# Tiles 4 to 7 of a folded adapter-and-expert layer: each pair's product with the folded weights made of seven block products instead of eight

## The reference

```python
h      = x @ W + (x @ lora_A[idx]) @ lora_B[idx]          # per tile, rank 16
out    = h @ W_base.T + b_base
logits = h @ W_gate.T                                     # 8 experts
p      = top-2 of softmax(logits), made to sum to 1; route_w puts it back on 8 experts
delta  = ((h @ A[e].T) * route_w[e]) @ B[e].T, summed over e   # rank 16 per expert
result = x + out + delta
```

## Time and profile before

| | us |
|---|---|
| median of 3 runs (lowest, highest) | 65.82 (65.64, 66.08) |
| span of the profiled execution, first to last instruction | 64.2 |
| TensorE busy | 60.7 |
| VectorE busy | 36.7 |
| ScalarE busy | 25.7 |
| GpSimd busy | 17.9 |
| granted TensorE clock, share of full speed | 1.00 |

### The profile page before, as it was taken

How to read it: one execution, slowest core, us unless ns; L and a number is a source line. 1 busy time by engine, 2 the same in 40 slices (tenths; PEclk the granted TensorE clock), 3 DMA queues, 4 the chain that set the end, 5 groups by cost and what they waited for, 6 DMA issues and landing times.

```text
span 64.2 us, 1268 instructions
## 1 busy us (share of the span) xinstructions
PE 60.7 (95%) x418; PEld 59.6 (93%) x418; DVE 36.7 (57%) x131; ACT 25.7 (40%) x73; POOL 17.9 (28%) x41
## 2 busy tenths in 40 slices
PE   4979999999999999999999999999999999999950
PEld 4969999999999999999999999999999999999940
DVE  0948599915799747020788748990477240467120
ACT  1752899507294270001163436611272011173620
POOL 1000899899988802030020301230000000000000
DMA  0799999702988102232332323800017000008044
GB/s 0 209 328 308 367 406 411 278 3 48 323 295 309 31 0 42 61 70 60 70 70 57 63 66 65 309 31 5 0 48 278 0 10 0 0 28 299 0 163 163
DMA packets 5048, 8.46 MB, mean 132 GB/s; under 512 B 1057, under 2 KB 1569, under 8 KB 5042
## 3 DMA queue, kind: packets, MB, share of 16 engines
q1 hardware_dynamic: 4370, 7.57, 36.6%
q0 software_dynamic: 384, 0.56, 2.4%
q10 hardware_dynamic: 288, 0.27, 1.2%
HBM read 5.26 MB, written 2.10 MB: 115 GB/s over the span
## 4 chain that ended last, share of the span: by engine, by line
PE 90%; DMA 5%; ACT 1%; issue 0%
PE bank L487 22%; PE bank L489 22%; PE bank L488 22%; PE bank L495 8%; PE bank L497 6%; DMA w_raw<-fold_in 5%; PE bank L573 2%; PE bank L538 2%; PE bank L554 2%; PE bank L544 2%; PE bank L577 1%; PE bank L528 1%; ACT y_out L333 1%; PE bank L584 1%; PE bank L588 1%
## 5 line engine op out<-in xcount | busy, mean ns | idle before, releaser
L487 PE MATMUL bank<-cl_hi,x_hi 128*128 128x408 f32 x32 | 11.4, 356 | 0.0
L489 PE MATMUL bank<-cl_hi,x_lo 128*128 128x408 f32 x32 | 11.2, 349 | 0.0
L488 PE MATMUL bank<-cl_lo,x_hi 128*128 128x408 f32 x32 | 11.1, 348 | 0.0
L487 PE MATMUL bank<-cr_hi,x_hi 128*128 128x256 f32 x32 | 9.6, 301 | 0.0
L489 PE MATMUL bank<-cr_hi,x_lo 128*128 128x256 f32 x32 | 9.0, 282 | 0.0
L488 PE MATMUL bank<-cr_lo,x_hi 128*128 128x256 f32 x32 | 9.0, 282 | 0.0
L261 POOL CAST cl_hi<-lora_raw 128x64 fp32r<-128x64 f32 x8 | 1.9, 239 | 16.8 <-PE bank L489 16.8
L448 DVE MAX8 top_val<-bank 128x8 f32<-128x8 f32 x8 | 1.4, 169 | 8.7 <-PE bank L538 8.7
L487 PEld LDWEIGHTS bank<-cr_hi,x_hi 128*128 128x128 f32 x32 | 6.1, 190 | 0.2
L228 POOL DMA_DIRECT2D lora_raw<-lora x8 | 4.5, 564 | 6.2 <-issue 6.1
L487 PEld LDWEIGHTS bank<-cl_hi,x_hi 128*128 128x128 f32 x32 | 6.0, 188 | 0.1
(11 more groups left out here) (99 smaller groups left out, 149.3 us busy)
## 6 DMA issues: line engine op xcount, KB each, us to landing
x_raw<-x_t SPq DMA_DIRECT2D x8, 256.0 KB, 4.5
out<-y_out SPq DMA_DIRECT2D x7, 256.0 KB, 2.1
w_raw<-fold_in SPq DMA_DIRECT2D x4, 256.0 KB, 5.1
w_raw<-fold_in SPq DMA_DIRECT2D x3, 324.0 KB, 5.2
bw_rows<-bw_hi SPq DMA_DIRECT2D x16, 40.5 KB, 2.0
lora_raw<-lora POOLq DMA_DIRECT2D x8, 64.0 KB, 3.9
bw_rows<-bw_lo SPq DMA_DIRECT2D x8, 40.5 KB, 2.1
ffn_b_raw<-ffn_b SPq DMA_DIRECT2D x1, 256.0 KB, 6.1
```

The lines of the kernel that those rows point to most:

```text
L487: nc.tensor.matmul(out, a_hi, b_hi, start=first, stop=False, skip_group_check=True)
L488: nc.tensor.matmul(out, a_hi, b_lo, start=False, stop=False, skip_group_check=True)
L489: return nc.tensor.matmul(out, a_lo, b_hi, start=False, stop=last, skip_group_check=True)
```

## The change

Pairs 2 and 3 (tiles 4, 5 and 6, 7) are multiplied by Strassen's scheme. For a pair with tiles a and b, the features are cut in halves 1 and 2 and the output columns in halves, so that `[a1 a2; b1 b2]` meets `[B11 B12; B21 B22]`. `M5 = (a1+a2) B22`, `M4 = b2 (B21-B11)`, `M3 = a1 (B12-B22)`, `M2 = (b1+b2) B11`, `M1 = (a1+b2)(B11+B22)`, `M6 = (b1-a1)(B11+B12)`, `M7 = (a2-b2)(B21+B22)`. Each is two chunks of three matmuls. M5, M4, M3, M2 carry the gate, h and adapter columns along (408 columns, in the left banks); M1, M6, M7 have 256 columns. Tile a's left bank now holds the right half of its output.

The operands that this needs are made on the chip. ScalarE copies the raw folded weights out of the banks (`copy_left_raw`, `copy_right_raw`), VectorE makes the differences `X4` and `X3`, GpSimd the sums `SUM1`, `SUM7`, `SUM6` (`sum_c`), the mixed x quarters (`sum_x`: three of 256 columns, and then one of 512 in place), and the adapters' A columns for a pair (`split_la_pair`). All are split into hi and lo. The results are combined with copies of M5 and M4 and with sums `e`, `z`, `u1`, `u2` and `add_u` on GpSimd and VectorE. The bias moves from GpSimd to ScalarE and VectorE, and its rows go out as eight DMAs on SyncE's queue.

```diff
+SEVEN = (2, 3)
+X5, X3, C01, C23, X4 = range(5)
+SUM1, SUM6, SUM7 = range(3)
...
+            def sum_x(q):
+                x, k = quarters(x_raw, q), SEVEN.index(q)
+                pool.wait_ge(x_loaded[2 * q], DMA)
+                pool.wait_ge(x_loaded[2 * q + 1], DMA)
+                pool.wait_ge(x_lo_done, 4)
+                nc.gpsimd.tensor_tensor(x_mix[k][:, SUM1], x[:, 0], x[:, 3], ALU.add).then_inc(x_mixed, 1)
+                nc.gpsimd.tensor_tensor(x_mix[k][:, SUM6], x[:, 2], x[:, 0], ALU.subtract).then_inc(x_mixed, 1)
+                nc.gpsimd.tensor_tensor(x_mix[k][:, SUM7], x[:, 1], x[:, 3], ALU.subtract).then_inc(x_mixed, 1)
+                pool.wait_ge(x_mixed, 3 * k + 3)
+                nc.gpsimd.tensor_tensor(x[:, 1:3], x[:, 1:3], x[:, 0:4:3], ALU.add).then_inc(x_summed, 1)
...
+            def split_x_inner(q):
+                act.wait_ge(x_summed, SEVEN.index(q) + 1)
+                nc.scalar.copy(quarters(x_hi, q)[:, 1:3], quarters(x_raw, q)[:, 1:3]).then_inc(x_hi_done, 1)
...
+            copy_xa_t(3)
+            copy_left(4)
+            copy_right(4)
+            exp_top(6)
+            copy_left(5)
+            copy_right(5)
+            exp_top(7)
+            split_hw(6)
+            split_hw(7)
...
+            gate(6)
+            sum_u1(3)
+            gate(7)
+            split_hw(6)
+            split_hw(7)
...
+            def M4(q):
+                pe.wait_ge(yl_done, 2 * q - 2)
+                if q == SEVEN[0]:
+                    pe.wait_ge(x4_lo_done, 1)
+                seven_left(2 * q + 1, 2, X4, q, True).then_inc(m4_done, 1)
+
+            def M3(q):
+                if q == SEVEN[0]:
+                    pe.wait_ge(x3_lo_done, 1)
+                    pe.wait_ge(x3_gh_done, 2)
+                pe.wait_ge(m5_copied, SEVEN.index(q) + 1)
+                seven_left(2 * q, 0, X3, q, False).then_inc(left_done, 1)
...
             Lora_left(1)
-            Left(4, ALL)
+            M5(2)
+            M4(2)
             T2(2)
-            Left(5, ALL)
+            M3(2)
+            M2(2)
             T2(3)
...
+            M7(2)
+            T1(3)
+            M6(2)
+            Lora_left(3)
+            Lora_right(2, (4, 5))
+            Delta(4)
+            M1(3)
+            Delta(5)
+            M7(3)
+            T2(6)
+            M6(3)
+            Lora_right(3, (6, 7))
+            T2(7)
+            Delta(6)
+            Delta(7)
```

More of the change, by code:

```diff
@@ L170, in right, with quarters, xd, xd_chunk @@
             return right_bank[t % 2][:, 0:HALF]
+        def quarters(x, q):
+            return x[:, 2 * q:2 * q + 2].rearrange("p t (h c) n -> p (t h) (c n)", h=2)
+        def xd(x, q):
+            return quarters(x, SEVEN.index(q))[:, 0:3]
+        def xd_chunk(x, q, which, c):
+            return xd(x, q)[:, which, c * P:(c + 1) * P]
+        def xd_free(q):
+            return 2 * SEVEN.index(q) + 1
+        def mix(q):
+            return part(x_flat, 2 * q * D, 3, HALF)
+        def la_slot(q):
+            return slice(0, R) if q % 2 == 0 else slice(OWN, OWN + R)
+        def la_own(q):
+            return own_cols(q)
         def fold_right(i):
@@ L244, in gpsimd_program, with split_la @@
             pool.wait_ge(even_zeros, 1)
[L246 to L258, removed]
+            def split_la(t):
                 if t >= 2:
@@ L287, in scalar_program @@
             split_x(1)
+            act.wait_ge(bias_loaded, DMA)
+            nc.scalar.copy(bias_hi[:], bias_raw[:]).then_inc(bias_hi_done, 1)
             act.wait_ge(lora_loaded, NT * DMA)
@@ L298, in scalar_program @@
                 nc.scalar.copy(cl_hi[:, i, LORA_LEFT], bank[i][:, 0:LEFT]).then_inc(cl_hi_done, 1)
[L299 to L303, removed]
+            act.wait_ge(cr_summed, 1)
+            nc.scalar.copy(cr_hi[:].rearrange("p c n -> p (c n)"), bank[4][:]).then_inc(cr_hi_done, 1)
@@ L518, in Right, with seven_left @@
                         pe.wait_ge(cr_lo_done, c // 2 + 1)
-                    product(right(t), x_hi[:, t, c, :], x_lo[:, t, c, :], cr_hi[:, c, :], cr_lo[:, c, :], c == 0, False)
+                    b_hi = cr_hi[:, c, :] if c < 2 else c_hi[:, X5, c - 2, A_RIGHT]
+                    b_lo = cr_lo[:, c, :] if c < 2 else c_lo[:, X5, c - 2, A_RIGHT]
+                    product(right(t), x_hi[:, t, c, :], x_lo[:, t, c, :], b_hi, b_lo, c == 0, False)
+            def seven_left(t, c0, which, q, first):
+                own = la_own(q)
+                for c in range(2):
+                    mm = product(left(t)[:, own], x_hi[:, t if which in (X5, X3) else 2 * q + 1, c0 + c, :],
+                                 x_lo[:, t if which in (X5, X3) else 2 * q + 1, c0 + c, :],
+                                 c_hi[:, which, c, own], c_lo[:, which, c, own], first and c == 0, False)
+                return mm
```

479 lines of the change are left out of this document (385 added, 94 removed).

## The result

The changed kernel took a median of 71.65 us (71.10 to 72.57, 4 runs) where the kernel before, beside it, took 65.73 (65.07 to 66.08, 4 runs): a ratio of 1.096, 95% interval 1.085 to 1.108. The forecast was 67.2 us in a range of 65.5 to 68.4: the sign was right, the loss was more than four times the one forecast, and the time lies outside the range. The profiled execution took 71.1 us with a span of 69.9, so its rows are compared with those of the 64.2 us span of before.

The account below looks back on a forecast made before the run. The number of matmuls on TensorE was taken as the bound. Twelve fewer (-1.44 us) plus A 1.6, B 0.43, C 0.15, D 0.55, E 0.14 gave +1.43 on 65.82: 67.2 us, range 65.5 to 68.4.

Parts of the forecast that it names:

- term A: First adapter product: ScalarE's adapter rows stand behind a cast waiting for GpSimd's x sums, slowed by VectorE's subtractions; +1.6 us.
- Term D: Transpose T2 of tile 7 at the end: later exponential of tile 6 and a new sum between gates; +0.55 us.
- B: M4 of tiles 4 and 5 waits for tile 1's left half to be copied out of its bank; +0.43 us.
- C: M3 of tiles 4 and 5 waits for ScalarE's copy of M5, behind tile 3's exponential; +0.15 us.
- E: After T2 of tile 7, only Delta of tile 6 stands before tile 7's low part is needed; +0.14 us.
- Rival 2: GpSimd is held up and slow at 2.9 ns a column, making A 2.8 us: 68.5 us; chance 0.15.

Follow-up runs that it names:

- the faster kernel: Changed kernel with gate steps moved off SBUF-only operands, GpSimd's weight sums out of the first gates, and lists reordered: 64.61 us (0.983), again 64.13 (0.985).
- sums alone: Kernel before plus three unread GpSimd sums of 512 columns, started when the first adapter product is done: 69.47 us against 65.45.
- the same sums beside the other gate: Kernel before plus the same three unread GpSimd sums, with the one-hot made from and in the bank and no difference step: 65.66 us, 1.006.
- The run with the end's old order: Changed kernel with tile 6's exponential ahead of the copy of tile 4's right half, and `u1` behind `split_hw(6)`: 70.87 us, 1.087.
- order alone: Seven-product kernel with every list in the order of the faster kernel, but with the old gate: 66.39 us, 1.021.

## Why the prediction was wrong

**The bound and the matmuls were right.** TensorE's matmuls set the time, and twelve of them are worth 1.44 us: the faster kernel shows 1.65 between its first and last tile product. (The pages count 418 and 406 matmuls, not 412 and 400; the difference is the forecast's.)

**The step that failed is in term A's second half: "After it, GpSimd's list goes on ... sums for the weights".** It asked only whether those sums are ready for the products that read them. It did not ask which VectorE instructions run beside them, though the same text knew that the two engines disturb each other, and it priced that as a share of time lost by GpSimd (0.57 us per us), never as a delay of VectorE. The row that it rested on the earlier trace rows shows both sides: the subtraction that lasted 0.95 instead of 0.68 us was taken as a reason to lower the price, and not as a price of its own. A share of overlap also hides the size: a step of 0.17 us that starts just behind the start of a sum of 1.27 costs 1 us, however small a share of the time the step itself takes up. The runs with sums alone (3.0 us later at `hw`, three steps) and with the same sums beside the other gate (nothing) show this mechanism. It made T2 of tiles 0 and 1 late by 3.43 us.

The Trainium skill ("SBUF — State Buffer", Who interferes with whom) states this rule: a VectorE instruction that has two SBUF inputs, or runs in a mode that uses both its ports, contends with a GpSimd instruction that reads SBUF, and the one that issues second is blocked until the first is done. The rows agree: a short step that comes behind the start of a sum of 1.27 us lasts 1.18 to 1.24 and ends with it. The same section of the Trainium skill counts `tensor_scalar` among the operations that can use both ports (the difference step, held to 1.20 and 1.25), and frees an instruction with at most one SBUF input outside that mode (here the steps with an operand in a bank, 0.18 to 0.23 us, and `RECIPROCAL`, 0.16 or 0.17).

**Term D failed by the same cause.** What it did see was right: the exponential behind one more copy moved the reciprocal by 0.36 us (0.34 forecast; 1.63 after its `MAX8` instead of 1.27), and `u1` took 0.33 (0.33). One matmul more, which was to take 0.12 off, took off next to nothing: from `Lora_left` of tiles 6 and 7 TensorE is free for T2 of tile 7 after 4.50 us (59.46 to 63.96), before after 4.51 (54.76 to 59.27), since before it lost 0.12 on the way (two starts of 256 columns take 0.36 there, 56.66 to 57.02). That makes 0.69, where 0.55 was forecast. The other 0.80 of the 1.49 are the three steps held by GpSimd's last sums (0.32, 0.21 and 0.34 longer, not all of it on the path). The run with the end's old order gave back 0.7 of 1.60 and left the holds.

**Term A was mis-sized**, 1.14 instead of 1.6. The mechanism was as described: ScalarE's adapter rows (30.92) came behind the cast that waited 2.58 us for GpSimd's sums and the negated gate columns. The sums lost 1.5 us (5.0 from 25.02 to 30.02, where the four sums of the second pair, with no VectorE subtraction beside most of them, took 3.5), near the 1.73 forecast, but they began 0.18 us earlier and ended at 30.02, not 30.5.

**B, C and E were right**: 0.44, 0.17 and 0.14 against 0.43, 0.15 and 0.14. The three are waits of a kind that the trace of before shows directly: an instruction's place in a list and its length.

**The rivals** all moved inside the same terms; none had VectorE held by GpSimd, so no range that they set could reach 71.65. Rival 2 (68.5) was nearest in size and wrong in its cause: undisturbed, GpSimd's sums took 0.73 and 1.27 us, as the forecast took them (0.72 and 1.25). Its 2.8 us for A, the upper end of the range, come to 3.0 by the terms given (0.8 for the slower columns, 2.3 for the overlap, less the 0.12), which would have changed nothing here.

## What to carry to other kernels

Work that moves to an idle GpSimd is not free for VectorE: lay GpSimd's new list beside VectorE's, and price each VectorE instruction from SBUF to SBUF that meets it (here only `RECIPROCAL` went free) at up to the length of one GpSimd instruction; a chain of short dependent steps pays that once per step. Two remedies are to be had: put GpSimd's long instructions where VectorE has none of those steps on the path, or give the short steps an operand in a bank. The first freed the first two gates here, but in a kernel with GpSimd at work almost everywhere it was not enough (66.39 us by order alone); with the second it was (64.13). And when a wait is taken away, look at once for the next one behind it: after the changed kernel's own waits four others had to go before the 1.44 us came to light.

## What the runs showed of the hardware

- The hold in both directions: VectorE's steps 0.17 to 1.24 us beside a sum of 1.27; GpSimd's 256-column sums 0.74 to 1.19 and 1.47 us beside subtractions of 512 and 784 columns. The one that starts second waits: in the faster kernel VectorE's `x_lo` (34.47) kept its 0.69 us, and GpSimd's sum that started at 34.69 took 1.62. `RECIPROCAL`, from SBUF to SBUF with one input of one element, had 0.16 or 0.17 us beside a sum that was under way (32.23 and 33.78, in the run of the sums beside the new gate).
- TensorE's clock after a long wait. In the run of the sums alone, TensorE stood idle for 2.32 us up to 35.39, and then the granted clock was 0.55 (windows: start and end, length, busy time of PE, PEld, DVE, ACT and POOL, granted clock, DMA):

```profile
30.00:35.30 5.30, 3.08 (x18) 2.73 (x17) 4.49 (x10) 0.30 (x2) 4.27 (x5) 1.00 0.31 68
35.30:38.90 3.60, 3.51 (x12) 3.45 (x13) 2.48 (x14) 1.49 (x5) 0.16 (x1) 0.55 0.25 56
```

  There matmuls of 408 columns start every 0.34 us instead of 0.186, that is at the lower level, 1.2 GHz: ten of them cost 1.5 us, a third of that run's loss. The profiled execution of the changed kernel kept 1.00 after it had stood idle for 2.39 us; that of the same kernel with the end's order stood idle for 2.38 us up to 37.62, and then the granted clock was 0.51 from 37.50 to 41.00, with 0.34 us between the same starts. So a long wait can cost more than itself, and does not always.
